# Attention and two convolutions on one core: queries and keys projected as three fp16 products, two blocks ahead of the values

## The reference

```python
xn = group_norm(x, gn_weight, gn_bias)
qkv = jnp.einsum('oc,bchw->bohw', qkv_weight, xn) + qkv_bias[None, :, None, None]
q, k, v = jnp.split(qkv, 3, axis=1)
attn = jnp.einsum('bhdk,bhdq->bhkq', q, k) / np.sqrt(hd)
attn = jax.nn.softmax(attn, axis=-1)
out = jnp.einsum('bhkq,bhdq->bhdk', attn, v).reshape(b, c, h, w)
out = jnp.einsum('oc,bchw->bohw', proj_weight, out) + proj_bias[None, :, None, None]
return x_in + out
```

## Time and profile before

| | us |
|---|---|
| median of 3 runs (2878.61 to 2879.64) | 2878.78 |
| profiled execution | 2875.61 |
| its span, first to last instruction | 2873.6 |

### The profile page before, as it was taken

The page is one execution under the profiler, slowest core; times in us unless marked ns, Lnnn a source line. Parts: engine busy times, 40 slices in busy tenths (PEclk is TensorE's granted clock), DMA queues, the critical chain, the costliest instruction groups (busy, mean ns, idle before and its releaser), DMA issues. The chain is left out here.

```text
span 2873.6 us, 43432 instructions
## 1 busy us (share of the span) xinstructions
PE 2773.8 (97%) x17060; PEld 1011.4 (35%) x17060; DVE 2106.7 (73%) x2496; ACT 1415.1 (49%) x1493; POOL 2014.4 (70%) x1192
## 2 busy tenths in 40 slices
PE   5999999999999999999999999989999999899898
PEld 2333333334333333334333333343333333344343
DVE  5788888727788888457888888277778885598785
ACT  3455555554555555544555555545555555254342
POOL 2688888894888888855888888948888888400022
PEclk9999999999999999999999999999999999999999
DMA  5100000001000000041000000000000000421022
GB/s 218 50 1 1 1 1 1 1 1 65 1 1 1 1 1 1 1 148 50 1 1 1 1 1 1 1 30 1 1 1 1 1 1 1 151 81 61 20 97 88
DMA packets 26818, 78.26 MB, mean 27 GB/s; under 512 B 1920, under 2 KB 2176, under 8 KB 25600
## 3 DMA queue, kind: packets, MB, share of 16 engines
q1 hardware_dynamic: 25648, 73.01, 7.2%
q10 hardware_dynamic: 976, 2.63, 0.3%
HBM read 58.86 MB, written 16.78 MB: 26 GB/s over the span
## 5 line engine op out<-in xcount | busy, mean ns | idle before, releaser
L540 POOL TENSOR_TENSOR acc_pool<-acc_pool,prob 128x512 f32<-128x512 f32 (+1 forms) x992 | 1780.6, 1795 | 294.8 <-ACT prob L609 173.6
L609 ACT ACTIVATE prob<-ps,exp_scale 128x1024 f32<-128x1024 f32 x1024 | 1088.0, 1110 | 980.2 <-PE ps L776 974.0
L867 DVE TENSOR_REDUCE m_part<-ps 128x2 f32<-128x1024 f32 x1024 | 1246.3, 1222 | 433.7 <-PE ps L730 409.8
L760 PE MATMUL ps<-prob,vals 128*64 128x512 f32 x4096 | 991.1, 605 | 0.0
L760 PEld LDWEIGHTS ps<-prob,vals 128*64 128x64 f32 x4096 | 248.8, 136 | 501.7 <-issue 363.8
L730 PE MATMUL ps<-k_hi,q_hi 64*128 64x512 f16 x2048 | 391.1, 383 | 15.9 <-DVE m_part L867 9.6
L776 PE MATMUL ps<-m_rows,shift 64*128 64x512 f16 x2048 | 389.1, 376 | 2.9 <-DVE m_rows L894 2.9
L771 PE MATMUL ps<-q_hi,k_hi 64*128 64x512 f16 x2048 | 389.9, 377 | 0.0
L771 PE MATMUL ps<-q_lo,k_hi 64*128 64x512 f16 x2048 | 389.0, 376 | 0.0
L771 PE MATMUL ps<-q_hi,k_lo 64*128 64x512 f16 x2048 | 389.0, 376 | 0.0
L936 DVE TENSOR_TENSOR ps<-ps,prob 128x512 f32<-128x512 f32 x480 | 331.5, 691 | 72.4 <-ACT prob L609 72.4
(11 more groups left out here) (112 smaller groups left out, 1455.4 us busy)
## 6 DMA issues: line engine op xcount, KB each, us to landing
xt<-in_x SPq DMA_DIRECT2D x32, 512.0 KB, 4.4
xf<-in_x SPq DMA_DIRECT2D x4, 2048.0 KB, 16.5
xn<-in_x SPq DMA_DIRECT2D x16, 512.0 KB, 7.1
x_scratch<-y_tile SPq DMA_DIRECT2D x16, 512.0 KB, 5.2
rows<-x_scratch SPq DMA_DIRECT2D x8, 576.0 KB, 5.1
rows<-x_scratch SPq DMA_DIRECT2D x8, 544.0 KB, 4.6
xt<-x_scratch SPq DMA_DIRECT2D x4, 1024.0 KB, 5.2
y_tile<-x_scratch SPq DMA_DIRECT2D x4, 1024.0 KB, 5.1
```

Source lines behind the costliest of these rows:

```text
L540: nc.gpsimd.tensor_tensor(acc[:, part], acc[:, part], tile[:, part], ALU.add).then_inc(pool_add, 1)
L609: nc.scalar.activation(prob[:, n % PBUF], g.ps_s[:, kt % 2].rearrange("p h n -> p (h n)"), ACT.Exp, scale=g.exp_scale[:]).then_inc(exp_don ...
L760: last = mm(g.ps_o[own[h], :], vals[:, kt, own[h]], prob[:, n % PBUF, h * TB:(h + 1) * TB], start=(kt == 0), stop=(kt == KT - 1))
L867: v.tensor_reduce(m_part[:, block % 2, :, u], source, AX.X, ALU.max).then_inc(mx_used, 1)
```

## The change

- Keys and queries: `product` makes three fp16 products a channel block, w_hi x_hi, w_hi x_lo and w_lo x_hi, six matmuls of 512 columns for two channel blocks. Values stay fp32.
- The parts: weights are scaled by `wscale`, then `w_hi` is their fp16 copy (ScalarE) and `w_lo` the rest (VectorE). `x_hi` (ScalarE) and `x_lo` are the same of `xn`, in `HS` = 3 slots. In pair 0 ScalarE and VectorE do it for blocks 0 to 2 at the start, VectorE scaling the weights; in the other pairs ScalarE scales the weights in the last but two query block, makes `x_hi` in the last but one, and VectorE makes `w_lo` and `x_lo` in the last. For blocks 3 to 7 ScalarE makes `x_hi` and GpSimd `x_lo` within the stage.
- The input is scaled by 64 over its bound (`rx`) in `gn_a` and `gn_b`; the prologue computes the scales with more small instructions. The evacuations lose their `scale`.
- The order: step 0 makes keys and queries of blocks 0 and 1, and each step up to 5 keys and queries of block step+2, so that steps 6 and 7 have the values only. The places of maxima are now 2, 1, 2, 2 in step 0, 1, 2, 2 in steps 1 to 5 and 2 in steps 6 and 7; `STAGE_UNITS` moves one pair of them.
- The normalization of blocks 4 to 7 is shared: channel block 0 on ScalarE, 1 on GpSimd.
- In a pair's last query block VectorE adds the halves of tiles 11 to 31 (`LAST_HALVES`), and ScalarE copies their sum after the last exponential.
- `wmid` of the second convolution gets memory of its own, since `wmid` in the shared memory is halved.

```diff
-STAGE_UNITS = (first_units(0) + first_units(1) + first_units(2) + ahead((0, 1)) + first_units(3) + ahead((2,)) +
-               first_units(4) + ahead((3,)) + first_units(5) + first_units(6) + first_units(7))
-VISITS = [(0, 2, 2)] + [(1, 2, 2)] * 5 + [(0, 2, 2), (0, 2, 1)]
+STAGE_UNITS = (first_units(0) + first_units(1) + first_units(2) + ahead((0, 1)) + first_units(3) + first_units(4) +
+               ahead((2, 3)) + first_units(5) + first_units(6) + first_units(7))
+VISITS = [(2, 1, 2, 2)] + [(0, 1, 2, 2)] * 5 + [(0, 0, 0, 2), (0, 0, 0, 2)]
...
+LAST_HALVES = list(range(11, KT))
...
+            for j in range(2):
+                step(v.tensor_scalar(g.wscale[:, j], xnb[:], g.fscale[:, j:j + 1], 1.0 / XRANGE, ALU.mult, ALU.mult))
+            step(v.tensor_scalar(g.wscale[:, 2], xnb[:], 1.0 / XRANGE, None, ALU.mult))
...
+                step(v.tensor_tensor(g.gn_a[:, s], g.gn_a[:, s], rx[:], ALU.mult))
+                step(v.tensor_tensor(g.gn_b[:, s], g.gn_b[:, s], rx[:], ALU.mult))
...
+            def split_x(it0, n):
+
+                pool.wait_ge(x_hi_ready, it0 + n + 1)
+                pool.wait_ge(x_lo_ready, it0 + n)
+                nc.gpsimd.tensor_tensor(x_lo[:, n % HS], xn[:, n % XS], x_hi[:, n % HS],
+                                        ALU.subtract).then_inc(x_lo_ready, 1)
...
-                            split_k(it0, 0)
-                            split_q(it0, 0)
-                            split_k(it0, 1)
-                            split_k(it0, 2)
-                        else:
-                            if step + 2 < NB:
-                                split_k(it0, step + 2)
-                            split_q(it0, step)
+                            for n in range(2):
+                                split_k(it0, n)
+                                split_q(it0, n)
+                        if step + HS < NB:
+                            split_x(it0, step + HS)
+                        if step + 2 < NB:
+                            split_k(it0, step + 2)
+                            split_q(it0, step + 2)
...
+            for n in range(HS):
                 for c in range(CB):
-                    normalize_first(0, s, c)
+                    normalize(0, n, c)
+                split_x(0, n)
+                if n == 0:
+                    split_weights(0)
+            for c in range(CB):
+                normalize(0, HS, c)
...
+            def product(into, j, kb):
+
                 for c in range(CB):
-                    last = mm(g.ps[:, 1], wst[:, c, 0, :], xn[:, kb % XS, c, :], start=(c == 0), stop=(c == CB - 1))
-                last.then_inc(q_done, 1)
+                    for w, x_part in ((w_hi, x_hi), (w_hi, x_lo), (w_lo, x_hi)):
+                        last = mm(into, w[:, c, j, :], x_part[:, kb % HS, c, :], start=(c == 0 and x_part is x_hi and w is w_hi),
+                                  stop=(c == CB - 1 and w is w_lo))
+                return last
...
                             project_k(b, hp, 1)
                             if hp:
                                 column_sums(it0 - 1)
-                            project_k(b, hp, 2)
-                        else:
-                            if step + 2 < NB:
-                                project_k(b, hp, step + 2)
+                            project_q(it0, 1)
                             first_maxima(it0, visit_units(step, 0))
-                            project_q(it0, step)
-                        first_maxima(it0, visit_units(step, 1))
+                        if step + 2 < NB:
+                            project_k(b, hp, step + 2)
+                            first_maxima(it0, visit_units(step, 1))
+                            project_q(it0, step + 2)
+                            first_maxima(it0, visit_units(step, 2))
                         project_v(b, it0, step)
-                        first_maxima(it0, visit_units(step, 2))
+                        first_maxima(it0, visit_units(step, 3))
...
+                    if last and it + 1 < 2 * B * NB:
+                        if group == 0:
+                            split_weights((it + 1) // NB)
+                        elif group <= HS:
+                            split_x((it + 1) // NB, group - 1)
```

More of the change, by code:

```diff
@@ L130, with halves @@
 SUMS_AT = 2
+def halves(it):
+    return LAST_HALVES if it % NB == NB - 1 else DVE_HALVES
 def halves_until(it, kt):
-    return it * len(DVE_HALVES) + sum(t <= kt for t in DVE_HALVES)
+    return sum(len(halves(i)) for i in range(it)) + sum(t <= kt for t in halves(it))
 class Shared:
@@ L413, in sb @@
             return ctx.enter_context(nc.sbuf_tensor(name, shape, dt))
+        w_hi, w_lo = (sb(n, [P, CB, 2, P], F16) for n in ("w_hi", "w_lo"))
+        x_hi, x_lo = (sb(n, [P, HS, CB, TB], F16) for n in ("x_hi", "x_lo"))
         k_hi, k_lo, q_hi, q_lo = (sb(n, [P, N], F16) for n in ("k_hi", "k_lo", "q_hi", "q_lo"))
@@ L595, in copy_v, with softmax @@
                                      ACT.Copy).then_inc(v_copied, 1)
-            def softmax(it, first, last, pair_after):
+            def softmax(it, first, last, weights_after, input_after):
                 for kt in range(KT):
@@ L689, in project_k @@
                     pe.wait_ge(yk_ready, it0 + kb)
-                for c in range(CB):
-                    last = mm(g.ps[:, 0], wst[:, c, 1, :], xn[:, kb % XS, c, :], start=(c == 0), stop=(c == CB - 1))
-                last.then_inc(k_done, 1)
+                product(g.ps[:, 0], 1, kb).then_inc(k_done, 1)
             def project_q(it0, kb):
@@ L872, in maxima_of, with scale_weights, split_weights, split_x @@
                     maximum(it0, unit, g.ps_max)
+            def scale_weights(pair):
+                dve.wait_ge(g.w_staged, 16 * (pair + 1))
+                for c in range(CB):
+                    for j in range(3):
+                        v.tensor_scalar(wst[:, c, j], wst[:, c, j], g.wscale[:, j, c:c + 1], None,
+                                        ALU.mult).then_inc(w_scaled, 1)
+            def split_weights(pair):
+                dve.wait_ge(w_hi_ready, pair + 1)
+                v.tensor_tensor(w_lo[:], wst[:, :, 0:2, :], w_hi[:], ALU.subtract).then_inc(w_lo_ready, 1)
+            def split_x(pair, n):
+                dve.wait_ge(x_hi_ready, pair * NB + n + 1)
+                dve.wait_ge(x_lo_ready, pair * NB + n)
+                v.tensor_tensor(x_lo[:, n % HS], xn[:, n % XS], x_hi[:, n % HS], ALU.subtract).then_inc(x_lo_ready, 1)
             def first_maxima(it0):
@@ L923, in add_half @@
             def add_half(it, kt):
[L925 removed]
+                if kt not in halves(it):
                     return
```

146 lines of the change are left out of this document (93 added, 53 removed).

## The result

| | us |
|---|---|
| after, median of 4 runs (2860.25 to 2861.61) | 2861.11 |
| before beside it, median of 4 runs (2878.61 to 2879.64) | 2878.90 |
| ratio, 95% interval | 0.9937 [0.9924, 0.9949] |
| profiled executions, before and after | 2875.61, 2861.23 |
| their spans | 2873.6, 2859.4 |

Faster by 17.8 us in the medians and by 14.2 us in the spans of the two profiled executions, where 27.6 were forecast. 2861 lies inside the range and 10 us above the forecast. One execution among those of the experiments was slow (2994.25 us at a mean clock of 0.921, in the run with lead-in maxima moved, late splits and the thinner end) and is in no ratio.

The account below looks back on a forecast made before the run. TensorE, busy 97% of the span, was taken as the bound. Gains of 2.9 (pair 0), 7.9 each (pairs 1 and 3) and 8.9 (pair 2), together 27.6 us, gave 2848.0; the runs' median is 3.2 higher, so 2851; range 2838 to 2866.

Parts of the forecast that it names:

- The products: Keys and queries in projection stages: six fp16 matmuls at 0.216 us each, 1.29 us against 1.91.
- The step, 6.34 us: Steps 1 to 5 of a stage: a loop over VectorE's reduces sets 6.34 us, above TensorE's bare work of 5.75.
- rival A: Projection stages: TensorE stays the bound, a step is 5.75, no clock falls; gain 42 us, 2837; chance 0.12.
- The chain of splits: GpSimd and ScalarE input splits within a stage: a 6.5 us loop, x_lo 2.3, run three times; costed at 0.
- Stage end: From the values of step 6, 8.2 us; keys of block 3 to max rows 39.9, gain 9.2 and 9.4 a stage.
- Lead-in, pair 0: Prologue and first steps: first keys at 43.1, keys of block 3 at 58.8 against 52.53, a loss of 6.3 us.
- Lead-in, pairs 1 and 3: Start of these stages: sums at 641.0, bank free at 647.2, 1.3 us added for lower clock; loss 1.5 each.
- Pair 2: Its stage has no column sums in the lead-in; keys of block 3 come 0.3 later, gain 8.9 us.
- The blocks: Query blocks: VectorE's new work could cost GpSimd 0 to 10.5 us in three last blocks; taken as 0.
- Rival B: Last blocks: VectorE's two-input work holds GpSimd; gain 17 us, 2862, or 2856 for half of it; chance 0.22.
- Rival D: Inside stages: small waits drop TensorE to 1.2 GHz, a step costs 11.3 us; slower than before, 2900 if half; chance 0.07.

Follow-up runs that it names:

- lead-in maxima moved, late splits and the thinner end: Kernel after with three edits: step 0's maxima moved, last-block splits in groups 9 to 12, last four maxima three and one; 2853.99 us, 0.9919.
- lead-in maxima moved: Kernel after with step 0's maxima moved behind block 2's products (one before its keys, three after queries, three after values); 2864.0 us, 0.9948.
- late splits: Kernel after with VectorE's w_lo and x_lo of a pair's last block moved from groups 0 to 3 to groups 9 to 12; 2854.74 us, 0.9918.
- the thinner end: Kernel after with three maxima in step 6 and one in step 7 of a stage, instead of two and two; 2858.87 us, 0.9932.
- a maximum amid the values: Kernel after with the first of the two maxima behind the values placed after two of their four tiles; 2861.75 us, 0.9941.
- lead-in maxima moved and splits late: Kernel after with two edits: step 0's maxima moved behind block 2's products, and last-block splits in groups 9 to 12; 2854.71 us, 0.9921.
- early sums: Kernel after with column sums of pairs 1 and 3 two products earlier, behind the keys of block 0; 2852.79 us, 0.9911.
- fp32 products: Kernel after with the old fp32 products of keys and queries in the new order, splits made but unused; 2891.79 us, 1.0047.
- no last halves: Kernel after with the last block's half sums put back to the other blocks' list (11 to 26, not 11 to 31); 2864.68 us, 0.9957.
- the last: Kernel after with last-block splits in groups 9 to 12 and column sums behind the queries of block 0 in pairs 1 and 3; 2851.24 us, 0.9902.
- score products first: Kernel after with score products of the first two key tiles ahead of the max rows; 2860.07 us, 0.9938. With late splits and early sums: 2852.31 us, 0.9907.

## Why the prediction was right in kind and 10 us short

- **The products.** Right: they carry the whole gain. Without them the change is slower than the kernel before (2891.79 us, ratio 1.0047).
- **The step, 6.34 us.** Measured 6.38, and the loop that sets it is the one forecast: 0.15 behind the reduce (0.11), 0.32 for the maximum and the turn, 1.98 for the values, 0.43 to the next reduce, three reduces in 3.49, 6.37 in all. Wrong was the bare work beside it, 6.2 us instead of 5.75: the 1.29 of six products left out the turn in front of a maximum (1.40), and the 0.22 and 0.43 of the maxima the turn back (0.32 and 0.57). So the loop adds 0.2 and not 0.6, and rival A's 5.75 was never to be had; the run with a maximum amid the values, with 6.48 of bare work, bears that out.
- **The chain of splits.** Right: x_lo on GpSimd takes 2.13 (2.3 forecast), and no keys wait for it inside a stage.
- **Stage end.** Forecast 39.9 from the keys of block 3 to the max rows, measured 39.95 in pair 0 (58.22 to 98.17) and 39.8 in pair 1.
- **Lead-in, pair 0.** K0 at 42.71 (43.1), keys of block 3 at 58.22 (58.8), gain 3.4 (2.9). The 0.5 is a slip: the forecast's own terms, 53.6 + 1.3 + 1.0 + 2.0 + 0.4, make 58.3. That the queries of block 2 start at 53.55 is partly luck: ScalarE had their bank evacuated by 52.66, its pieces standing 0.57 us apart and not 0.74, and TensorE came to them behind its own work.
- **Lead-in, pairs 1 and 3.** Column sums at 641.0 and bank at 647.2 as forecast. The term mis-sized is the 1.3 us for the lower clock: the products that the order puts behind the wait ran half as fast for longer, 2.8 us in pair 1 and 1.6 in pair 3. The walk is also 0.5 us longer than forecast without any fall: with the scores first, keys of block 3 come 17.25 behind K0, where 16.8 were forecast. Gains 6.0 and 7.2 for 7.9.
- **Pair 2.** 8.86 for 8.9.
- **The blocks.** The step that failed: "I take 0, since no row shows one slowing the other." Rival B was right in kind, at two thirds of its price: 6.7 us for 10.5. My argument against it, that the splits run in the first four groups and the waits came later, was mistaken; GpSimd loses some 3 us there (0.9 and 1.0 on the two rows above, 0.3 and 0.8 on two full adds) and carries them on until `prob` has no free slot, three groups later. The run with late splits shows it: 7.0 us back in these three stretches. The Trainium skill's "SBUF — State Buffer", section "Who interferes with whom", had said that a VectorE instruction with two SBUF inputs contends with a GpSimd instruction that reads SBUF. The trace after agrees: 2.58 for 0.69, 2.14 for 1.26. By the same section an instruction with at most one SBUF input, outside its 2-port modes, does not contend, and the trace agrees there too: the half sums (PSUM and `prob`) take 0.68 to 0.70 us beside a busy GpSimd.
- **The start of attention.** Not in the sum at all: 4.3 us. I had counted the last reduce in the stage's end, and not that TensorE waits there for longer than before and starts attention at the lower clock. Rival D looked for the fall inside the steps, where this trace has none, and not at the stage's edges (its own step adds up to 11.2 us, not 11.3). "TensorE: Matmul & The Clock Gate", section "A second HAM failure mode: psum-queue depth-cycling", in the Trainium skill, speaks of small idle gaps between groups of matmuls. The trace after doesn't show that: with a gap of about 0.2 us a step the clock stays up, and each of its six falls in the attention layer stands behind one long wait (2.59 to 3.38 us). The fall behind three waits of 0.68 to 0.79, in the run with lead-in maxima moved and splits late, comes nearer to it, but the same three waits stood in other stages without a fall.

By size: blocks 6.7, start of attention 4.3, lead-ins 2.6, against 0.5 more in pair 0: 13.1 of the 13.4 us between 27.6 and 14.2. The first of these is taken back by an edit (late splits); in the lead-ins the early sums shorten the stages of pairs 1 and 3 by 5.6 and 4.4 us. No edit took back the start of attention in all pairs: that a fall costs the time is shown, since rows to first values is 7.14 wherever the clock stays up and 7.87 or more wherever it falls, but what lets it fall is not.

What stays open is when the clock falls. At the start of attention, a wait of 2.6 to 2.7 us was followed by a fall every time, in 32 starts of eight kernels (the one after, and the runs with fp32 products, late splits, lead-in maxima, no last halves, lead-in maxima with late splits, early sums, and the last). A wait of 1.87 was followed by one in no pair of the kernel before, in three of four with the thinner end, and in two of four both in the run with a maximum amid the values and in the one with lead-in maxima moved, splits late and the thinner end. The three waits of 1.2 to 1.5 that score products first bring were followed by a fall in all eight starts of two kernels. What differs is that the kernel before still has queries to project in steps 6 and 7; whether that thinner work matters, the rival of the thinner end, was not tested by itself.

Waits of 3.38 in a lead-in had a long fall twice, a short one six times and none three times. The executions of one kernel spread over 0.7 to 8 us, and in the widest spread the mean granted clock goes with it (2857.53 us at 0.992, 2865.66 at 0.989, lead-in maxima moved); one execution of each was traced, so differences of 1 to 3 us between spans carry this scatter. Not tried: a kernel whose last reduces are shared out so that the stage ends without a wait.

## What to carry over

Where a change moves work to an engine that has time, ask what the engine next to it is doing meanwhile, and over how many groups a lag of its queue is carried before someone waits; here moving four instructions by nine groups gave back 6 us. When a projected stall is priced, price also the work that stands right behind it, for here it ran at the clock that the stall left; putting the short dependency (the column sums) two products earlier was worth more than any reordering of the work behind it. And where the length of a step comes out right, the terms that didn't set it have still to be checked row by row: here the bare work was 0.5 us off.

## What was not expected of the hardware

- A turn between matmuls of 64 rows and of 128 rows costs about 0.1 us of TensorE's time each way (0.31 and 0.32 between starts where equal fp16 matmuls stand 0.22 apart).
- Contention between VectorE and GpSimd slows both, and unevenly: w_lo takes 0.69 us alone, 2.58 beside full adds and 0.70 to 0.73 beside half adds, where the add beside it took 1.53 instead of 1.27; beside x_lo such an add took 2.06.
- TensorE's granted clock fell to 0.50 behind waits of 1.9 to 3.4 us, and three times behind three waits of 0.7 to 0.8 us in a row, in some stages and not in others, with the same instructions around.
